# Value matmuls of the first attention: one unit at a time, four units behind their scores, in place of sets of four heads

## The reference, cut to what matters

```python
q = (xn @ q_w + q_b).reshape(B, L, H, hd)      # B=8, L=512, H=16, hd=8
k = (xn @ k_w + k_b).reshape(B, L, H, hd)
v = (xn @ v_w + v_b).reshape(B, L, H, hd)
scores = jnp.einsum('bqhd,bkhd->bhqk', q, k) * hd ** (-0.5)
scores = jnp.where(causal[None, None], scores, -jnp.inf)
attn = jax.nn.softmax(scores, axis=-1)
attn_out = jnp.einsum('bhqk,bkhd->bqhd', attn, v).reshape(B, L, Dm) @ o_w + o_b
```

## Time and profile before

| | |
|---|---|
| Median of 3 runs | 2040.51 us (2033.99 to 2044.25) |
| The profiled execution | 2044.78 us |
| its span, first to last instruction | 2043.1 us |
| mean granted TensorE clock | 0.782 |
| Mixer stage, first to last unit of attention | about 185 to 1232 us |
| Values: matmul rows on `PT,Vb` | 1024 rows |
| Largest busy shares of the span | PE 85%, DVE 68%, ACT 53%, POOL 41% |

### The profile page before, as it was taken

How to read it: one execution, slowest core, us unless ns; L and a number is a source line. 1 busy time by engine, 2 the same in 40 slices (tenths; PEclk the granted TensorE clock), 3 DMA queues, 4 the chain that set the end, 5 groups by cost and what they waited for, 6 DMA issues and landing times. The chain is left out here.

```text
span 2043.1 us, 21887 instructions
## 1 busy us (share of the span) xinstructions
PE 1742.4 (85%) x7090; PEld 952.8 (47%) x7090; DVE 1394.9 (68%) x2071; ACT 1079.6 (53%) x1784; POOL 841.3 (41%) x863
## 2 busy tenths in 40 slices
PE   4958979979878879888799887887999999989878
PEld 3334423333333333333333333645877877763673
DVE  1596766767767767767667833858776868766876
ACT  3734444444454454454444436646778787852107
POOL 1363545535535444455455523112122222226762
PEclk8865676676776776767766768988999999985879
DMA  2111101101111111111011002110111111100001
GB/s 74 68 57 58 53 23 61 52 31 54 46 53 42 49 59 36 36 63 50 24 61 52 22 1 62 31 49 14 52 47 38 46 42 47 42 21 0 1 1 41
DMA packets 61678, 84.74 MB, mean 41 GB/s; under 512 B 6600, under 2 KB 32062, under 8 KB 61566
## 3 DMA queue, kind: packets, MB, share of 16 engines
q1 hardware_dynamic: 61466, 83.31, 13.1%
q10 hardware_dynamic: 100, 0.03, 0.0%
HBM read 74.38 MB, written 8.78 MB: 41 GB/s over the span
## 5 line engine op out<-in xcount | busy, mean ns | idle before, releaser
L993 PE MATMUL bank<-QK 48*128 48x128 bf16 (+7 forms) x1024 | 303.9, 381 | 110.7 <-DVE Mx L1242 67.7
L1682 POOL TENSOR_TENSOR dBx<-dtx,Bb 128x512 f32<-128x512 f32 x256 | 321.4, 1277 | 16.1 <-DMA Bb<-b_dram 9.6
L1553 ACT ACTIVATE bank<-dtv,alog 128x512 f32<-128x512 f32 x256 | 176.3, 690 | 263.1 <-DVE hst L1262 262.3
L1242 DVE TENSOR_REDUCE Mx<-bank 128x1 f32<-128x384 f32 (+3 forms) x352 | 220.2, 632 | 137.2 <-PE bank L993 135.0
L1295 DVE TENSOR_TENSOR hl<-lsq,hh 128x512 fp32r<-128x512 f32 x320 | 257.0, 814 | 81.8 <-ACT hh L1569 73.5
L1662 POOL TENSOR_SCALAR_AFFINE_SELECT PT<-PT 128x256 f32<-128x256 f32 (+1 forms) x320 | 118.0, 372 | 465.7 <-ACT PT L1509 465.4
L1262 DVE TENSOR_TENSOR_SCAN hst<-bank,dBx 128x512 f32<-128x512 f32 x256 | 297.9, 1204 | 4.5 <-POOL dBx L1682 4.5
L1509 ACT ACTIVATE PT<-bank 128x512 f32<-128x512 f32 x320 | 185.0, 591 | 208.4 <-PE bank L993 206.7
L1566 ACT ACTIVATE lsq<-bank,vcol 128x512 f32<-128x512 f32 x320 | 218.7, 692 | 112.8 <-DVE hl L1295 69.4
L1180 DVE SCALAR_TENSOR_TENSOR yT<-bank,bc,yT 128x256 f32<-128x256 f32 x480 | 203.8, 478 | 90.5 <-PE bank L1096 90.5
L993 PEld LDWEIGHTS bank<-QK 48*128 48x128 bf16 (+1 forms) x1024 | 72.1, 100 | 355.0 <-issue 161.7
(11 more groups left out here) (247 smaller groups left out, 2531.3 us busy)
## 6 DMA issues: line engine op xcount, KB each, us to landing
Bb<-b_dram SPq DMA_DIRECT2D x128, 256.0 KB, 3.4
stage<-w_rows SPq DMA_DIRECT2D x64, 256.0 KB, 3.2
parts<-part SPq DMA_DIRECT2D x16, 384.0 KB, 2.8
QK<-parts SPq DMA_DIRECT2D x64, 96.0 KB
QK<-parts SPq DMA_DIRECT2D x64, 64.0 KB
stage<-in_L_ffn_We_dram SPq DMA_DIRECT2D x16, 256.0 KB, 3.2
hst<-in_L_attn_x_dram SPq DMA_DIRECT2D x8, 256.0 KB, 5.5
QK<-parts SPq DMA_DIRECT2D x64, 32.0 KB
```

The lines of the kernel that those rows point to most:

```text
L993: return engine.matmul(o, l, r, start=start, stop=stop, tile_position=pos, skip_group_check=True)
L1242: engine.tensor_reduce(Mx[:, it["u"] % 2, qi, h:h + n], o[:, 0:P * (qi + 1) * n].rearrange("p (i c) -> p i c", i=n), AX.X, ALU.max).then_i ...
L1553: engine.activation(bank[4 + h][:], dtv[:, b % 2, h, :], ACT.Exp, scale=alog[:, h, n:n + 1]).then_inc(sems["act_da"], 1)
L1682: engine.tensor_tensor(dBx[:, sl, h], dtx[:, b % 2, h], Bb[:, sl], ALU.mult).then_inc(sems["pool_dbx"], 1)
```

## The change

`weigh` now takes one unit. It is put into the list as soon as four younger units have been put there (`settle(LAG)`, LAG = 4), so after every unit of scores there is one unit of values. The blocks of a unit are issued in the unit's own order and no longer sorted over four heads. `PT` has 6 slots. In the matmuls of the row maxima, only the first head's matmul of a bank now carries the start flag.

```diff
-NPT = 10
+NPT = 6
+LAG = 4
...
-    def weigh(b, g, units):
+    def weigh(b, g, parts, sl, x, y):
         k = 3
-        it = step("weigh", b=b, g=g, bank=k, free=free.get(f"b{k}"), ready=(r_v[b], [(x, y) for _, _, x, y in units]),
-                  blocks=sorted((kj, i, off, sl) for parts, sl, _, _ in units for i, kj, off in parts))
-        it["m"] = up("pe_av")
-        for _, sl, _, _ in units:
-            free[f"PT{sl}"] = it["m"]
+        it = step("weigh", b=b, g=g, parts=parts, sl=sl, bank=k, free=free.get(f"b{k}"), ready=(x, y, r_v[b]))
+        it["m"] = free[f"PT{sl}"] = up("pe_av")
         return it["m"]
...
     def settle(n):
         while len(late) > n:
-            b, g, units, end = late.pop(0)
-            m = weigh(b, g, units)
+            b, g, parts, sl, x, y, end = late.pop(0)
+            m = weigh(b, g, parts, sl, x, y)
...
-            sets = [[(i, 0, 0)] for i in range(4)], [[(i, 1, 0), (i, 3, 384)] for i in range(4)], [[(i, 2, 0), (i + 2, 2, 256)] for i in range(2)]
-            for parts_of in sets:
-                units = []
-                for parts in parts_of:
...
-                    units.append((parts, sl, it["x"], it["y"]))
-                    if len(units) == len(parts_of):
-                        late.append((b, g, units, parts_of is sets[2]))
-                    settle(1)
-                    yield
+            units = [[(i, 0, 0)] for i in range(4)] + [[(i, 1, 0), (i, 3, 384)] for i in range(4)] + \
+                [[(i, 2, 0), (i + 2, 2, 256)] for i in range(2)]
+            for parts in units:
...
+                late.append((b, g, parts, sl, it["x"], it["y"], parts is units[-1]))
+                settle(LAG)
+                yield
...
                         mm(o[:, kc * i:kc * i + kc], QK[64 * h:64 * h + 48, 0, s, a, P * qi:P * qi + P], QK[64 * h:64 * h + 48, 1, s, a, 0:kc],
-                           stop=False)
+                           start=(i == 0), stop=False)
...
-                    for kj, i, off, sl in it["blocks"]:
+                    for i, kj, off in it["parts"]:
                         n = T - P * kj
                         if kj == 0:
                             q.wait_ge(it["free"])
                         x = mm(o[32 * i:32 * i + 32, P * kj:T], Vb[:, b % 2, kj, 36 * g + 9 * i:36 * g + 9 * i + 32],
-                               PT[:, sl, off:off + n], start=(kj == 0), stop=(kj == 3), pos=(0, 32 * i))
+                               PT[:, it["sl"], off:off + n], start=(kj == 0), stop=(kj == 3), pos=(0, 32 * i))
```

More of the change, by code:

```diff
@@ L243, in attend @@
             g = 2 * hf + gg
-            sets = [[(i, 0, 0)] for i in range(4)], [[(i, 1, 0), (i, 3, 384)] for i in range(4)], [[(i, 2, 0), (i + 2, 2, 256)] for i in range(2)]
-            for parts_of in sets:
-                units = []
-                for parts in parts_of:
[L248 to L256, removed]
-                    units.append((parts, sl, it["x"], it["y"]))
-                    if len(units) == len(parts_of):
-                        late.append((b, g, units, parts_of is sets[2]))
-                    settle(1)
-                    yield
+            units = [[(i, 0, 0)] for i in range(4)] + [[(i, 1, 0), (i, 3, 384)] for i in range(4)] + \
+                [[(i, 2, 0), (i + 2, 2, 256)] for i in range(2)]
+            for parts in units:
+                k = take()
+                sl = pts[0] % NPT
+                pts[0] += 1
+                it = step("att", u=u, gg=gg, parts=parts, sl=sl, bank=k, free=free.get(f"b{k}"), ready=(r_mr[u], r_qk[u]),
+                          pt_free=free.get(f"PT{sl}"))
+                it["m"] = up("pe_sc")
+                it["x"] = free[f"b{k}"] = up("act_exp")
+                it["y"] = up("pool_sel")
+                m = it["m"]
+                late.append((b, g, parts, sl, it["x"], it["y"], parts is units[-1]))
+                settle(LAG)
+                yield
         free[f"QK{s}"] = m
```

## The result

The changed kernel took **2009.4 us** (median of 4 runs, 1993.3 to 2017.2) against 2039.8 us before on the same footing: ratio 0.984, 95% interval 0.981 to 0.988. So it is faster by 1.6%, where I had forecast 2152 us, slower by 5.5%. The range, 2035 to 2290 us, did not hold it. The case that happened is rival C, the clock that pays, to which I had given 0.12; but its price, 1951 us, was 58 us too low.

The account below looks back on a forecast made before the run. PE was taken as the bound at 1.2 GHz, with PE and DVE waiting for each other at 2.4 GHz. At 3.93 us a unit, 157.3 us a batch, 8 batches add 111 us to 2040.5: 2152 us, range 2035 to 2290.

Parts of the forecast that it names:

- rival C: Mixer stage: added work keeps the high clock 0.80 of the time, value matmuls vanish in PE's idle time; 1951 us, chance 0.12.
- Packing and its price on PE: Value matmuls: a lone head costs what four packed ones did; adds 1.22 us a unit at low clock, 0.66 at high.
- the other price in the prediction: Value matmuls: the Trainium skill's 2.38x for three column tiles puts one head at 1.48 us, the sum at +62 us.
- Between 0.40 and 0.76 I take 0.60: Mixer stage: more 128-row value work raises the share of time at 2.4 GHz from 0.40 to 0.60.
- The sign of the feedback and its reason: PE clock: more continuous value work with 128 rows raises the high-clock share above 0.40; narrow outputs do not prevent it.
- My upper guide: Last stage: PE busy 0.80 at clock 0.88, so 0.76 of the time at the high level, guiding the mixer's share.
- The slow unit, 5.32 us: Mixer stage at 1.2 GHz: PE is the bound and added work is paid in full, 4.10 + 1.22 us a unit.
- The fast unit, 3.35 us: Mixer stage at 2.4 GHz: the middle between 3.02 us (added work fully hidden) and 3.68 us (nothing hidden) a unit.
- 4.10 and 3.02 us: Kernel before, one batch: time per unit of attention at 1.2 and 2.4 GHz, with progress measured by DVE's busy time.
- The wait for the copy of bank 3: First value matmul of a group waits for the 0.59 us copy; costed at nothing, 19 us if wholly late.
- Slots and start flag: Six PT slots hold the five units under way, each free before its next exponential; start flag adds no instruction: nothing.
- Rival B: Mixer stage: the clock does not follow the added work, high-clock share stays 0.40; +231 us, 2271 us, chance 0.20.

Follow-up runs that it names:

- Pairs: Changed kernel with values weighed two units at a time, a pair following when two younger pairs are there, 8 PT slots: 1989.3 us, 1994.0 us in a second series.
- the clumped waste: Kernel before plus 20 useless 128-row matmuls a group, eight before the last unit of each of the first two sets, four in the third: 2013.5 us.
- the heads kept apart in old places: Kernel before, old order, with a full-width one-column matmul adding zero behind each head's value matmul (every second in key block 2): 2221.7 us.

## Why the prediction was wrong

- **Packing and its price on PE: right.** Lone heads cost 1.85 and 0.98 us against the 1.86 and 1.00 used, and not the 1.48 us of the other price in the prediction. PE busy per value row of 512 columns rose from 0.21 to 155.2/256 = 0.61 us, as said.
- **The step that failed: "Between 0.40 and 0.76 I take 0.60", the share of time at the high clock.** It came out at 747/965 = 0.77. With my own unit prices this alone gives 1 / (0.774/3.35 + 0.226/5.32) = 3.66 us a unit, 146.2 us a batch, +23 us instead of +111: 88 of the 142 us between +111 and the -31 us of the two spans. That would still be slower; the rest of the miss, and with it the sign, lies in the two unit prices below. The sign of the feedback and its reason were right: waste with narrow outputs raised the clock, waste of transposes did, waste with 48 rows didn't, each now shown by a run of its own. I failed to see that this feedback is worth more than the work that feeds it. The kernel of before was so short of 128-row work that 320 matmuls of pure waste already gained 1.6%. My upper guide, the last stage with 0.80 PE busy, is other work with waits of its own, and the mixer stage passed it: 0.77 here, and 822.51/965 = 0.85 in a run of 1993.0 us of the same changed kernel. The trace of before also holds a stretch at the full clock with PE 0.98 busy, which I did not weigh:

```profile
1700.00:1820.00 120.00, 117.59 (x501) 93.02 (x500) 95.91 (x132) 97.61 (x155) 28.65 (x21) 1.00 0.14 41
```

- **The slow unit, 5.32 us: too dear.** With the same 2.48 us of DVE work a unit as the measure, the changed kernel needs 2.48 x 217.71/112.94 = 4.78 us at the low clock. The kernel of before needs 2.48 x 591.93/370.81 = 3.96 us over the same stretch, so 0.82 us a unit was added where I had 1.22.
- **The fast unit, 3.35 us: too dear as well.** It is 2.48 x 747.29/577.89 = 3.21 us, against 2.48 x 373.08/304.85 = 3.03 us before: 0.17 of the 0.66 us a unit was exposed, and not the half that I had taken. PE at 0.90 busy beside DVE at 0.77 shows that PE can be filled further than the 0.7 of before let me think. Only where waste had already filled PE was more than half exposed (0.39 us, above). With the three measured values, 1 / (0.774/3.21 + 0.226/4.78) = 3.47 us, 138.7 us a batch, some -38 us against my one batch of 143.4 us. Over the same stretch as the new values the kernel of before takes 141.7 us a batch (40 x 2.48 x 965/675.66), which makes it -24 us; the spans say -31.
- **The measure itself is rough.** It takes for granted that attention and DVE's work advance together at both clocks. ACT's busy time on `PT` (100.51 us at the low and 61.58 us at the high clock before, 25.87 and 141.60 us now, 0.59 us an exponential) counts units directly and gives 3.47 and 3.57 us a unit before, 4.97 and 3.11 us now. So in the kernel of before the low stretches hold more attention than DVE's share says, and "4.10 and 3.02 us" was partly a difference in the mix of work. The shares 0.39 and 0.77 do not depend on it; how the rest of the miss divides between the two prices does, and stays open.
- **The wait for the copy of bank 3: in its bound.** I had cost it at nothing, at most 19 us; it is 12.7 us of PE idle time.
- **Slots and start flag: right**, nothing, by runs of their own.
- **Rival B** did not happen; what it describes is seen with other work, in the run with 48-row waste: the clock does not follow and the work is paid, 2220 us. **Rival C** is what happened, at a share of 0.77 and a fast unit of 3.21 us, which is under the 3.31 us at which I had put its turning point at a share of 0.80. The value matmuls did not vanish at 2.4 GHz, as its price of 1951 us had it. Its chance of 0.12 was too low, since I had weighed a slow change of 111 us as if the clock's answer could only soften it.
- **Still open:** how much of the clock's rise in the changed kernel comes from the added value work and how much from the even order, and what that order is worth by itself. Pairs (1989 us), the clumped waste (42 us over the spread one) and the heads kept apart in old places (2222 us) all fit with spacing helping; none isolates it from PE work of its own kind.

## What to carry to other kernels

Where PE is the bound at half its clock in a stage of short matmuls with few rows, ask first what would raise the clock, and only then what the added work costs: one head's 512 columns took 1.85 us at the low clock and 0.98 us at the high one. Look at the share of time at each level and not at busy time, which was 0.95 at the low clock here. Try it with waste before rebuilding anything: two useless 128-row matmuls a unit gave 3.3% here, more than the 1.6 to 2.7% of the change, and the same waste with few rows is the control. In this kernel it was better to keep the packing and spread the filler evenly: giving up the packing cost 89 us net where the waste already held the clock up.

## What the runs showed of the hardware that I had not expected

Two bf16 matmuls of 512 columns a unit moved the time by -68 us with 128-row operands and by +181 us with 48-row operands, at clocks of 0.92 and 0.64. Operands with 128 rows into only 32 array columns kept the clock at 0.89, and float32 transposes of 128x128 gave a clock of 0.906 over the span and the lowest time of all, 1959.9 us. In the stretches that were summed the granted clock was 0.50 or 1.00, so 1.2 or 2.4 GHz; what differed between kernels was the share of time at each. The 128-row operands here are an identity and a mask, the 48-row ones keys and queries, so whether their values play a part was not tried.
